# Four-bit rounding moved from GpSimd to VectorE, with more score banks and looser waits, in a transformer layer

## The chip, the cores and the metric

The program runs on all 8 cores of one Trainium2 chip. Each core computes one of the 8 sequences with all the weights, and the cores exchange nothing. The metric is the device time of one launch in microseconds, taken on the slowest core; lower is better.

## The reference

For one sequence `x` of 2048 tokens by 1024 features the layer is attention after a layer norm, then a gated feed-forward block after a second layer norm, both with a residual:

```
x = x + attn(layernorm(x))          # 16 heads of 64, rotary, causal, softmax, Wo
h = silu(q(xn) @ q(wg).T) * (q(xn) @ q(wu).T)      # xn = layernorm(x), inner width 2816
x = x + q(h) @ q(wd).T
def q(v):                           # along the last axis, blocks of 16
    scale = max(max|v| / 6, 1e-12)
    idx = searchsorted([0.25,0.75,1.25,1.75,2.5,3.5,5.0], |v/scale|)
    return [0,0.5,1,1.5,2,3,4,6][idx] * sign(v) * scale
```

So three weight matrices are rounded once, and the normed input and the inner activation are rounded for every token.

## The kernel before

The kernel is written engine by engine: a scheduler object collects steps for each engine in the order in which the Python code adds them, each with the semaphore values it waits for, and every engine runs its own list strictly in that order. Nothing is reordered later.

The work runs in stages. Stage A (to about 130 us) norms the 16 token tiles of 128 tokens and transposes them. Stage B is attention, eight passes over pairs of heads. A pass loads its slice of the projection weights (`wstg`, SyncE queue), casts it on VectorE, multiplies 16 tiles on TensorE (line 482, banks `psA` and `psB`), applies the rotary factors on VectorE, and transposes. Then for each of its two heads and each of four blocks of 512 queries (`qb`) it walks over `4*qb + 4` key chunks: a score matmul (line 588, banks `psC` and `psD` in turn), an exponential on ScalarE (lines 605 and 641) into one of four slots of `PT`, on the last four chunks a multiply by the causal mask on VectorE (lines 614 and 650), and a value matmul (lines 621 and 656). A score matmul runs one chunk ahead of the value matmul.

Between these steps `e1_pump` (after the projections, after `qb` 1, 2 and 3, and at the end of each head) puts one job of the weight rounding: 60 jobs of 128 x 1024 and 8 of 128 x 768, which are read from memory into `wfE`, rounded in `quant_chain`, and written back by a DMA on the GpSimd queue. The read of the next job is issued on the SyncE queue once the chain before has ended.

Stage C multiplies by `Wo` tile by tile (line 768), with the output in `psO` for even tiles and in `psA`/`psB` for odd ones, adds the residual on VectorE (lines 785, 787), takes the statistics of the second norm and stores the tile. Stage E loads the rounded weights and transposes them into SBUF. Stage F is the feed-forward block, 16 token tiles: load `x_t`, norm, two chains of 128 x 512, transposes and a copy `xqT_t`, then six chunks of the inner width, five of 512 and one of 256. A chunk has eight gate and eight up matmuls (1042, 1050), two ScalarE reads of them (1061, 1067), the product `hmat` on VectorE (1073), and a chain. The tail of a chunk (transposes 1001, the copy `hqT_t` 1009, eight down matmuls into `psO`, 1020) is put behind the next chunk's gate and up matmuls, and behind its chain in the lists of ScalarE. At the end of the tile `x_t + psO` is formed (1090) and stored.

`quant_chain` is the helper behind all 68 chains of stage B and all 128 of stage F. On VectorE it takes the block maxima (154) while ScalarE takes absolute values (157), forms the scales (162 to 171) and the scaled magnitude `u` (178). Its step `c3A` (187 to 194) has seven comparisons of `u` with a threshold and the sign factor. GpSimd adds the seven results in six additions (200 to 214), and VectorE multiplies by scale and sign (221 to 237) when GpSimd is done.

Of the kernel before, what the change touches and what calls it, by code (L numbers as in the profile page):

```python
# [61 lines left out]
def build_nc(debug=False):  # L62
# [31 lines left out]
    R = "right"  # L94
# [18 lines left out]
    sPOOL = Sem(root.enter_context(nc.semaphore("sPOOL")))  # L113
# [33 lines left out]
    def quant_chain(bufs, F, src, soff, dst, doff, waits1, waits3):  # L147
        (qu, qt_, qa, qb_, qc_, sg, s2, bm, sh, rb, bmc, rb2, xsq, p6, p7) = bufs
# [50 lines left out]
        def pl1(g):
            g.tensor_tensor(qa[:, 0:F], qa.ap()[:, 0:F], qb_.ap()[:, 0:F],  # L200
                            Alu.add)
            g.tensor_tensor(qc_[:, 0:F], qc_.ap()[:, 0:F], qt_.ap()[:, 0:F],  # L202
                            Alu.add)
            return g.tensor_tensor(xsq[:, 0:F], xsq.ap()[:, 0:F],  # L204
                                   p6.ap()[:, 0:F], Alu.add)
        p1v = sch.add("gpsimd", pl1, waits=[(sDVE, va)], inc=sPOOL)

        def pl2(g):
            g.tensor_tensor(qa[:, 0:F], qa.ap()[:, 0:F], qc_.ap()[:, 0:F],  # L209
                            Alu.add)  # L210
            return g.tensor_tensor(xsq[:, 0:F], xsq.ap()[:, 0:F],  # L211
                                   p7.ap()[:, 0:F], Alu.add)
        p2v = sch.add("gpsimd", pl2, waits=[(sPOOL, p1v)], inc=sPOOL)
        p3v = sch.add("gpsimd", (lambda g: g.tensor_tensor(  # L214
            qa[:, 0:F], qa.ap()[:, 0:F], xsq.ap()[:, 0:F], Alu.add)),
            waits=[(sPOOL, p2v)], inc=sPOOL)
# [14 lines left out]
        vf = sch.add("vector", c3f, waits=[(sPOOL, p3v)], inc=sDVE)  # L231
# [11 lines left out]
    with root, nc.Block() as block:  # L243
# [59 lines left out]
        for t in range(NT):  # L303
# [49 lines left out]
            if t >= 2:  # L353
# [21 lines left out]
               for i in range(2)]  # L375
# [89 lines left out]
        for pr in range(NP):  # L465
# [109 lines left out]
            for hh in range(2):  # L575
                po = 64 * hh
                for qb in range(4):
# [5 lines left out]
                    for kc in range(nkc):  # L583
                        bk = sc_ctr % 2
# [13 lines left out]
                        if len(pend) >= 2:  # L598
# [104 lines left out]
                for g in range(2):  # L703
                    def t2s(te, g=g):
# [7 lines left out]
                    wt2 = [(sDVE, vnorm), (sACT, sACT.n)]  # L712
                    t2_prev_pe = sch.add("tensor", t2s, waits=wt2, inc=sPE)
                    sch.add("scalar", (lambda c, g=g, po=po, pr=pr: c.copy(
                        attnT.ap()[po:po + 64, pr, g * 1024:(g + 1) * 1024]
                        .rearrange("p (jj f) -> p jj f", f=128),
                        psT2.ap()[0:64, :]
                        .rearrange("p (jj f) -> p jj f", f=128))),
# [19 lines left out]
        for nh in range(2):  # L738
# [15 lines left out]
        obank = [(psO.ap()[:, 0:512], psO.ap()[:, 512:1024]),  # L754
                 (psA.ap()[:], psB.ap()[:])]
        for t in range(NT):
            r = t % 2
            ob0, ob1 = obank[t % 2]
# [5 lines left out]
            def omm(te, t=t, ob0=ob0, ob1=ob1):  # L764
                ins = None
                for nh, ob in ((0, ob0), (1, ob1)):
                    for pr in range(NP):
                        te.matmul(ob,
# [3 lines left out]
                    ins = te.matmul(ob, ones1.ap(),  # L772
# [4 lines left out]
            if t >= 2:  # L777
                waits.append((sDVE, epiC[t - 2]))
# [406 lines left out]
```

How the kernel before makes its waits and increments, by code:

```python
                def f(ctx):  # L50
                    for waits, emit, inc, amt in steps:
                        for sem, val in waits:
                            ctx.wait_ge(sem.h, val)
                        ins = emit(ctx)
                        if inc is not None:
                            ins.then_inc(inc.h, amt)
# [1039 lines left out]
        def final_wait(c):  # L1096
            c.wait_ge(sFO[0].h, final_out[0])
            return c.wait_ge(sFO[1].h, final_out[1])
```

## Time and profile before

| | |
|---|---|
| median of 3 runs | 5397.76 us (5396.99 to 5398.55) |
| the profiled execution | 5398.35 us |
| span of its slowest core, from the first to the last instruction | 5396.7 us |
| spans of all cores | 5380.7 to 5396.7 us |
| busy: TensorE / VectorE / ScalarE / GpSimd | 1941.2 / 1925.0 / 1140.3 / 1875.3 us |

Busy time is that of instructions on the engine; TensorE's is modelled, as its matmuls overlap. No engine is busy for more than 36% of the span, so the shares alone don't say what sets the time: the order of the waits does. Stages by the clock of the span: A to 130 us, B to 2861, C to 2960, E to 3129, F to the end.

### The profile page before, as it was taken

Reading aid. Unit: us, or ns where it says so; the run is one execution under the profiler, and the core shown is the slowest. Engines: PE = TensorE matmul, PEld = TensorE weight load, DVE = VectorE, ACT = ScalarE, POOL = GpSimd, SP = SyncE. Lnnn points to the kernel's source line nnn. Section 1 sums busy time; section 2 is a strip of 40 time slices with the busy share of each in tenths; the row PEclk is TensorE's granted clock in tenths of the full one; section 3 lists DMA queues with packets and bytes.
Section 4 is the critical chain, followed back from the end, with each engine's and each line's share of the span. In section 5 each row is a group of like instructions: output and inputs, shape, how many; then the busy total and the mean of one; then the engine's idle time right before and its main releaser. Section 6 shows DMA issues by size and latency. Waiting matters only on the chain.

```text
span 5396.7 us, 31104 instructions; the slowest of 8 cores (5380.7 to 5396.7 us)
## 1 busy us (share of the span) xinstructions
PE 1941.2 (36%) x6864; PEld 712.1 (13%) x6864; DVE 1925.0 (36%) x4494; ACT 1140.3 (21%) x1936; POOL 1875.3 (35%) x1280
## 2 busy tenths in 40 slices
PE   1532334333323344333436333333333333333333
PEld 0101001011010011110102311111111111111111
DVE  2333332333323324243234034433334333344333
ACT  4321222212212223132222321111111111111111
POOL 0243442433434423334230034343343433443433
PEclk9656556555565565655657566666666666666666
DMA  2000000010000000000004300000000000000000
GB/s 80 22 24 30 18 24 24 24 35 18 24 29 18 23 29 22 28 22 21 23 23 161 108 24 4 8 8 8 8 8 8 8 8 8 8 8 8 8 8 4
DMA packets 49107, 131.59 MB, mean 24 GB/s; under 512 B 8610, under 2 KB 16930, under 8 KB 48803
## 3 DMA queue, kind: packets, MB, share of 16 engines
q1 hardware_dynamic: 39012, 95.51, 6.2%
q0 software_dynamic: 9920, 34.09, 1.6%
q8 instruction: 68, 1.11, 0.1%
q14 instruction: 107, 0.88, 0.1%
HBM read 95.50 MB, written 34.08 MB: 24 GB/s over the span
## 4 chain that ended last, share of the span: by engine, by line
POOL 34%; DVE 29%; PE 16%; issue 8%; ACT 7%; DMA 5%; DVEq 1%; POOLq 0%; ACTq 0%; SPq 0%
POOL qcA L214 3%; POOL qcA L209 3%; POOL qcA L200 3%; POOL qcAF L214 3%; POOL qcAF L209 3%; POOL qcAF L200 3%; POOL qxs L204 3%; POOL qxs L211 3%; POOL qcC L202 3%; POOL qxsF L204 3%; POOL qxsF L211 3%; POOL qcCF L202 3%; PE psO L621 2%; PE psA L482 2%; PE psB L482 2%
## 5 line engine op out<-in xcount | busy, mean ns | idle before, releaser
L200 POOL TENSOR_TENSOR qcA<-qcA,qcB 128x1024 f32<-128x1024 f32 (+1 forms) x68 | 154.1, 2266 | 1628.2 <-DVE qs L194 1628.2
L200 POOL TENSOR_TENSOR qcAF<-qcAF,qcBF 128x512 f32<-128x512 f32 (+1 forms) x128 | 152.7, 1193 | 1383.8 <-DVE qs2F L194 1383.8
L621 PE MATMUL psO<-PT,vaug 128*65 128x512 bf16 x576 | 360.2, 625 | 637.6 <-DVE PT L614 572.4
L221 DVE TENSOR_TENSOR qcCF<-qcAF,qshF 128x256 f32<-128x256 f32 (+1 forms) x128 | 52.3, 409 | 970.0 <-POOL qcAF L214 970.0
L221 DVE TENSOR_TENSOR qcC<-qcA,qsh 128x512 f32<-128x512 f32 (+1 forms) x68 | 46.0, 676 | 956.5 <-POOL qcA L214 956.5
L605 ACT ACTIVATE PT<-psC,nb 128x512 bf16<-128x512 f32 x320 | 219.9, 687 | 694.9 <-PE psC L588 694.6
L1001 PE MATMUL psT<-idn_b,hqb 128*128 128x128 bf16 x352 | 52.7, 299 | 804.3 <-DVE qbmF L154 720.4
L1020 PE MATMUL psO<-wdqT,hqT_t 128*128 128x512 bf16 x704 | 310.6, 618 | 77.2 <-ACT hqT_t L1009 63.2
L980 PE MATMUL psT<-idn_b,xqb 128*128 128x128 bf16 x128 | 16.2, 306 | 603.0 <-DVE xqb L237 603.0
L614 DVE TENSOR_TENSOR PT<-PT,mskb 128x512 bf16<-128x512 bf16 x192 | 77.8, 422 | 355.5 <-ACT PT L605 355.5
L482 PE MATMUL psA<-wqkvp,xlT 128*128 128x384 bf16 x512 | 108.0, 360 | 263.0 <-DVE wqkvp L471 262.9
L588 PE MATMUL psC<-QTr,KTr 64*128 64x512 bf16 x320 | 192.9, 603 | 10.7 <-ACT KTr L570 10.7
L621 PEld LDWEIGHTS psO<-PT,vaug 128*65 128x65 bf16 x576 | 75.1, 130 | 914.9 <-issue 914.9
L588 PE MATMUL psD<-QTr,KTr 64*128 64x512 bf16 x320 | 194.9, 609 | 0.0
L605 ACT ACTIVATE PT<-psD,nb 128x512 bf16<-128x512 f32 x256 | 176.0, 688 | 80.0 <-PE psD L588 79.4
L157 ACT ACTIVATE qxsF<-hmat 128x512 f32<-128x512 f32 x96 | 57.2, 596 | 625.4 <-DVE hmat L1073 625.4
L708 PE MATMUL psT<-idn_b,attokn 128*64 128x128 bf16 x256 | 33.0, 310 | 419.4 <-DVE attokn L699 399.3
L178 DVE TENSOR_TENSOR quE<-qxs,qr 128x1024 f32<-128x1024 f32 (+1 forms) x68 | 81.1, 1193 | 235.6 <-ACT qxs L157 234.0
L209 POOL TENSOR_TENSOR qcAF<-qcAF,qcCF 128x512 f32<-128x512 f32 (+1 forms) x128 | 152.7, 1193 | 18.9 <-POOL qxsF L204 0.9
L214 POOL TENSOR_TENSOR qcAF<-qcAF,qxsF 128x512 f32<-128x512 f32 (+1 forms) x128 | 152.7, 1193 | 18.3
L214 POOL TENSOR_TENSOR qcA<-qcA,qxs 128x1024 f32<-128x1024 f32 (+1 forms) x68 | 154.6, 2274 | 10.1 <-POOL qxs L211 0.5
L209 POOL TENSOR_TENSOR qcA<-qcA,qcC 128x1024 f32<-128x1024 f32 (+1 forms) x68 | 154.7, 2274 | 9.8
(184 smaller groups left out, 5034.4 us busy)
## 6 DMA issues: line engine op xcount, KB each, us to landing
wstg<-wqkv SPq DMA_DIRECT2D x8, 1536.0 KB, 8.8
wfE<-wg SPq DMA_DIRECT2D x22, 512.0 KB, 3.8
wfE<-wu SPq DMA_DIRECT2D x22, 512.0 KB, 3.9
x_a<-x SPq DMA_DIRECT2D x16, 512.0 KB, 3.5
wfE<-wd SPq DMA_DIRECT2D x16, 512.0 KB, 4.0
x_c<-x SPq DMA_DIRECT2D x16, 512.0 KB, 4.0
xscr<-x1b POOLq DMA_DIRECT2D x16, 512.0 KB, 3.6
x_t<-xscr SPq DMA_DIRECT2D x16, 512.0 KB, 3.9
```

The lines of the kernel that those rows point to most:

```text
L200: g.tensor_tensor(qa[:, 0:F], qa.ap()[:, 0:F], qb_.ap()[:, 0:F], Alu.add)
L202: g.tensor_tensor(qc_[:, 0:F], qc_.ap()[:, 0:F], qt_.ap()[:, 0:F], Alu.add)
L204: return g.tensor_tensor(xsq[:, 0:F], xsq.ap()[:, 0:F], p6.ap()[:, 0:F], Alu.add)
L209: g.tensor_tensor(qa[:, 0:F], qa.ap()[:, 0:F], qc_.ap()[:, 0:F], Alu.add)
L211: return g.tensor_tensor(xsq[:, 0:F], xsq.ap()[:, 0:F], p7.ap()[:, 0:F], Alu.add)
L214: p3v = sch.add("gpsimd", (lambda g: g.tensor_tensor(qa[:, 0:F], qa.ap()[:, 0:F], xsq.ap()[:, 0:F], Alu.add)), waits=[(sPOOL, p2v)], inc=s ...
L221: v.tensor_tensor(qc_.ap()[:, 0:F2].rearrange("p (b k) -> p b k", k=16), qa.ap()[:, 0:F2].rearrange("p (b k) -> p b k", k=16), sh.ap()[:, ...
L482: te.matmul(ps[:, 0:384], xlT.ap()[:, kc, t * 128:(t + 1) * 128], wqkvp.ap()[:, kc, :], start=(kc == 0), stop=False)
L588: return te.matmul(ps[:], KTr.ap()[po:po + 64, kc * 128:(kc + 1) * 128], QTr.ap()[po:po + 64, qb * 512:(qb + 1) * 512], start=True, stop=True)
L605: c.activation(PT[:, kcp % 4, :], ps[:], AFT.Exp, bias=nb12.ap(), scale=0.125)),
L621: return te.matmul(av_banks[abk], vaug.ap()[:, kcp, hh, :], PT[:, kcp % 4, :], start=(kcp == 0), stop=(kcp == nkc - 1), skip_group_check=True)
L1020: ins = te.matmul(psO[:, nh * 512:(nh + 1) * 512], hqT_t.ap()[:, j, :], wdqT.ap()[:, j, nh * 512:(nh + 1) * 512], start=(j == 0), stop=(j ...
```

## The change

It has five parts. (1) In `quant_chain` GpSimd's three steps are gone. `c3A` becomes `c3a` with two comparisons and the sign factor, and the other five thresholds are folded in by `scalar_tensor_tensor` instructions on VectorE, each of which compares `u` with an immediate and adds a second tensor; seven of them stand in four steps, each of which waits for the one before. The buffers `p6` and `p7` and the semaphore `sPOOL` go. (2) In attention the scores rotate over four banks (`psC`, `psD`, `psA`, `psB`), and the score matmuls run two chunks ahead. (3) The transposes in attention, and those in the feed-forward block, wait for the last ScalarE copy that read their bank, in place of the newest ScalarE step. (4) Stage C has one output bank pair, `psO`, for every tile, and one addition of 1024 columns in place of two of 512. (5) The final sum of stage F is written into new buffers `outb`, and the load of `x_t` no longer waits for the store of the tile two before.

```diff
-        def c3A(v):
+        def c3a(v):
             u = qu.ap()[:, 0:F]
             v.tensor_scalar(qa[:, 0:F], u, TH[0], None, Alu.is_gt)
-            v.tensor_scalar(qb_[:, 0:F], u, TH[1], None, Alu.is_gt)
-            v.tensor_scalar(qc_[:, 0:F], u, TH[2], None, Alu.is_gt)
-            v.tensor_scalar(qt_[:, 0:F], u, TH[3], None, Alu.is_gt)
-            v.tensor_scalar(xsq[:, 0:F], u, TH[4], 2.0, Alu.is_gt, Alu.mult)
-            v.tensor_scalar(p6[:, 0:F], u, TH[5], 2.0, Alu.is_gt, Alu.mult)
-            v.tensor_scalar(p7[:, 0:F], u, TH[6], 4.0, Alu.is_gt, Alu.mult)
+            v.tensor_scalar(qc_[:, 0:F], u, TH[4], None, Alu.is_gt)
             return v.tensor_scalar(s2[:, 0:F], sg[:, 0:F], 2.0, -1.0,
                                    Alu.mult, Alu.add)
...
-        p1v = sch.add("gpsimd", pl1, waits=[(sDVE, va)], inc=sPOOL)
...
+        def c3b(v):
+            u = qu.ap()[:, 0:F]
+            v.scalar_tensor_tensor(qb_[:, 0:F], u, TH[1], qa.ap()[:, 0:F],
+                                   Alu.is_gt, Alu.add)
+            return v.scalar_tensor_tensor(qt_[:, 0:F], u, TH[5],
+                                          qc_.ap()[:, 0:F],
+                                          Alu.is_gt, Alu.add)
+        vb = sch.add("vector", c3b, waits=[(sDVE, va)], inc=sDVE)
...
+        ve = sch.add("vector", (lambda v: v.scalar_tensor_tensor(
+            qa[:, 0:F], qt_.ap()[:, 0:F], 2.0, qb_.ap()[:, 0:F],
+            Alu.mult, Alu.add)), waits=[(sDVE, vd)], inc=sDVE)
...
-        vf = sch.add("vector", c3f, waits=[(sPOOL, p3v)], inc=sDVE)
+        vf = sch.add("vector", c3f, waits=[(sDVE, ve)], inc=sDVE)
...
-        sc_banks = [psC, psD]
+        sc_banks = [psC, psD, psA, psB]
...
+                    elif last_t2_evac[0]:
+                        waits.append((sACT, last_t2_evac[0]))
...
-                        bk = sc_ctr % 2
+                        bk = sc_ctr % 4
...
-                        if len(pend) >= 2:
+                        if len(pend) >= 3:
...
-                    wt2 = [(sDVE, vnorm), (sACT, sACT.n)]
+                    wt2 = [(sDVE, vnorm)]
+                    if last_t2_evac[0]:
+                        wt2.append((sACT, last_t2_evac[0]))
...
-        obank = [(psO.ap()[:, 0:512], psO.ap()[:, 512:1024]),
-                 (psA.ap()[:], psB.ap()[:])]
...
-            if t >= 2:
-                waits.append((sDVE, epiC[t - 2]))
+            if t >= 1:
+                waits.append((sDVE, epiC[t - 1]))
...
+            epiC[t] = sch.add("vector", (lambda v, t=t, r=r: v.tensor_tensor(
+                x1b[r][:], x_c[r][:], psO[:], Alu.add)), waits=epw, inc=sDVE)
...
-                wx.append((sFO[r], out_dma[t - 2]))
...
-            wtx = [(sDVE, q2), (sACT, sACT.n)]
+            wtx = [(sDVE, q2)]
+            if last_psT_evac[0]:
+                wtx.append((sACT, last_psT_evac[0]))
...
-                wth = [(sDVE, qh), (sACT, sACT.n)]
+                wth = [(sDVE, qh)]
+                if last_psT_evac[cset]:
+                    wth.append((sACT, last_psT_evac[cset]))
...
-                x_t[r][:], x_t[r][:], psO[:], Alu.add)), waits=epw, inc=sDVE)
-            out_dma[t] = dma("gpsimd", sFO[r], out_v[:, t, :], x_t[r][:],
+                outb[r][:], x_t[r][:], psO[:], Alu.add)), waits=epw, inc=sDVE)
+            out_dma[t] = dma("gpsimd", sFO[r], out_v[:, t, :], outb[r][:],
```

## Rows read from the trace of the kernel before

**Rows 1.** Busy time by stage, microseconds: B, then F (windows; the columns first).

```profile
core 7: us, PE busy (x) PEld busy (x) DVE busy (x) ACT busy (x) POOL busy (x), PEclk, DMA share, GB/s
130.00:2861.00 2731.00, 1035.51 (x3200) 320.44 (x3200) 943.71 (x1684) 697.94 (x1285) 956.95 (x476) 0.54 0.08 24
...
3129.00:5397.00 2268.00, 751.11 (x2720) 302.70 (x2720) 889.57 (x2544) 288.33 (x450) 909.67 (x784) 0.63 0.02 8
```

**Rows 2.** The page's chain that ended last, by engine.

```profile
POOL 34%; DVE 29%; PE 16%; issue 8%; ACT 7%; DMA 5%; DVEq 1%; POOLq 0%; ACTq 0%; SPq 0%
```

**Rows 3.** Groups on VectorE by line and shape: busy, mean ns | idle before, releaser.

```profile
L178 DVE TENSOR_TENSOR quF<-qxsF,qr2F 128x512 f32<-128x512 f32 x112 | 77.5, 692 | 20.4 <-DVE qr2F L171 19.2 <-ACT up L1067 1.0 <-ACT hqT_t L1009 0.2
L178 DVE TENSOR_TENSOR quE<-qxs,qr 128x1024 f32<-128x1024 f32 x60 | 73.5, 1225 | 229.2 <-ACT qxs L157 227.7 <-DVE qr L171 1.2 <-ACT PT L605 0.3
...
L221 DVE TENSOR_TENSOR qcCF<-qcAF,qshF 128x256 f32<-128x256 f32 x112 | 47.6, 425 | 893.9 <-POOL qcAF L214 893.9
...
L221 DVE TENSOR_TENSOR qcC<-qcA,qsh 128x512 f32<-128x512 f32 x60 | 41.5, 692 | 866.7 <-POOL qcA L214 866.7
```

**Rows 4.** One 128 x 512 chain in stage F (timeline): start, length, engine.

```profile
4021.27 0.69 DVE L178 TENSOR_TENSOR quF<-qxsF,qr2F 128x512 f32<-128x512 f32 x1 [0.17 <-ACT up L1067]
4022.14 0.43 DVE L187 TENSOR_SCALAR qcAF<-quF 128x512 f32<-128x512 f32 x1 [0.17 <-DVE quF L178]
4022.48 0.42 DVE L188 TENSOR_SCALAR qcBF<-quF 128x512 f32<-128x512 f32 x1
...
4024.92 1.26 POOL L200 TENSOR_TENSOR qcAF<-qcAF,qcBF 128x512 f32<-128x512 f32 x1 [17.91 <-DVE qs2F L194]
...
4032.74 0.43 DVE L221 TENSOR_TENSOR qcCF<-qcAF,qshF 128x256 f32<-128x256 f32 x1 [7.97 <-POOL qcAF L214]
```

**Rows 5.** VectorE in attention around one 128 x 1024 chain (timeline).

```profile
1277.91 1.21 DVE L154 TENSOR_REDUCE qbm<-wfE 128x64 f32<-128x1024 f32 x1
1279.23 0.20 DVE L162 TENSOR_SCALAR qbc<-qbm 128x64 f32<-128x64 f32 x1
...
1284.54 0.69 DVE L189 TENSOR_SCALAR qcC<-quE 128x1024 f32<-128x1024 f32 x1
...
1305.02 0.75 DVE L614 TENSOR_TENSOR PT<-PT,mskb 128x512 bf16<-128x512 bf16 x2
1307.67 0.43 DVE L614 TENSOR_TENSOR PT<-PT,mskb 128x512 bf16<-128x512 bf16 x1 [1.90 <-ACT PT L605]
1308.78 0.42 DVE L650 TENSOR_TENSOR PT<-PT,mskb 128x512 bf16<-128x512 bf16 x1 [0.68 <-ACT PT L641]
1309.23 1.22 DVE L154 TENSOR_REDUCE qbm<-wfE 128x64 f32<-128x1024 f32 x1
```

**Rows 6.** TensorE after the chain that lies behind qb 2 (timeline).

```profile
1113.93 0.61 PE L621 MATMUL psO<-PT,vaug 128*65 128x512 bf16 x1 [9.58 <-DVE PT L614]
```

**Rows 7.** One chunk of stage F, from chain end to chunk ready (timeline).

```profile
4034.29 0.68 DVE L1073 TENSOR_TENSOR hmat<-silu,up 128x512 f32<-128x512 f32 x1
4035.07 0.63 ACT L157 ACTIVATE qxsF<-hmat 128x512 f32<-128x512 f32 x1 [13.90 <-DVE hmat L1073]
...
4036.52 0.59 ACT L1009 COPY hqT_t<-psT 128x512 bf16<-128x512 bf16 x1 [0.82 <-PE psT L1001]
...
4037.36 3.57 PE L1020 MATMUL psO<-wdqT,hqT_t 128*128 128x512 bf16 x8 [0.93 <-DVE qr2F L171]
...
4045.36 0.69 ACT L1067 ACTIVATE up<-psB,rstd_all 128x512 f32<-128x512 f32 x1 [1.04 <-PE psB L1050]
```

**Rows 8.** TensorE in stage C, first matmuls of two successive tiles (timeline).

```profile
2894.66 1.90 PE L768 MATMUL psO<-wos,attnT 128*128 128x512 bf16 x8
...
2898.96 1.90 PE L768 MATMUL psA<-wos,attnT 128*128 128x512 bf16 x8
```

**Rows 9.** The 1024-column addition from psO, in stage F (timeline).

```profile
4112.40 1.22 DVE L1090 TENSOR_TENSOR x_t<-x_t,psO 128x1024 f32<-128x1024 f32 x1 [3.27 <-PE psO L1020]
```

**Rows 10.** DMA issues of the page: KB each, us to landing.

```profile
wfE<-wu SPq DMA_DIRECT2D x22, 512.0 KB, 3.9
```

More of the change, by code:

```diff
@@ L194, in c3A @@
             return v.tensor_scalar(s2[:, 0:F], sg[:, 0:F], 2.0, -1.0,
                                    Alu.mult, Alu.add)
-        va = sch.add("vector", c3A, waits=[(sDVE, v2)] + list(waits3),
+        va = sch.add("vector", c3a, waits=[(sDVE, v2)] + list(waits3),
                      inc=sDVE)
[L199 to L205, printed above, removed]
@@ L206, in quant_chain @@
-        p1v = sch.add("gpsimd", pl1, waits=[(sDVE, va)], inc=sPOOL)
[L208 to L216, printed above, removed]
+        def c3b(v):
[5 more added lines that the diff above has]
+                                          Alu.is_gt, Alu.add)
@@ new lines, in quant_chain, with c3c @@
+        vb = sch.add("vector", c3b, waits=[(sDVE, va)], inc=sDVE)
+        def c3c(v):
+            u = qu.ap()[:, 0:F]
+            v.scalar_tensor_tensor(qa[:, 0:F], u, TH[2], qb_.ap()[:, 0:F],
+                                   Alu.is_gt, Alu.add)
+            return v.scalar_tensor_tensor(qc_[:, 0:F], u, TH[6],
+                                          qt_.ap()[:, 0:F],
+                                          Alu.is_gt, Alu.add)
+        vc = sch.add("vector", c3c, waits=[(sDVE, vb)], inc=sDVE)
@@ new lines, in c3d @@
+        def c3d(v):
+            u = qu.ap()[:, 0:F]
+            v.scalar_tensor_tensor(qb_[:, 0:F], u, TH[3], qa.ap()[:, 0:F],
+                                   Alu.is_gt, Alu.add)
+            return v.scalar_tensor_tensor(qt_[:, 0:F], u, TH[6],
+                                          qc_.ap()[:, 0:F],
+                                          Alu.is_gt, Alu.add)
+        vd = sch.add("vector", c3d, waits=[(sDVE, vc)], inc=sDVE)
+        ve = sch.add("vector", (lambda v: v.scalar_tensor_tensor(
+            qa[:, 0:F], qt_.ap()[:, 0:F], 2.0, qb_.ap()[:, 0:F],
+            Alu.mult, Alu.add)), waits=[(sDVE, vd)], inc=sDVE)
@@ L711, in t2s @@
                         return ins
-                    wt2 = [(sDVE, vnorm), (sACT, sACT.n)]
+                    wt2 = [(sDVE, vnorm)]
+                    if last_t2_evac[0]:
+                        wt2.append((sACT, last_t2_evac[0]))
                     t2_prev_pe = sch.add("tensor", t2s, waits=wt2, inc=sPE)
[L714 to L718, printed above, removed]
+                    last_t2_evac[0] = sch.add("scalar", (
+                        lambda c, g=g, po=po, pr=pr: c.copy(
+                            attnT.ap()[po:po + 64, pr,
+                                       g * 1024:(g + 1) * 1024]
+                            .rearrange("p (jj f) -> p jj f", f=128),
+                            psT2.ap()[0:64, :]
+                            .rearrange("p (jj f) -> p jj f", f=128))),
                         waits=[(sPE, t2_prev_pe)], inc=sACT)
@@ L762, in build_nc, with omm @@
             wxd = dma("sync", sXC[r], x_c[r][:], x_v[:, t, :], waits=wx)
-            def omm(te, t=t, ob0=ob0, ob1=ob1):
+            def omm(te, t=t):
                 ins = None
-                for nh, ob in ((0, ob0), (1, ob1)):
+                for nh in range(2):
                     for pr in range(NP):
-                        te.matmul(ob,
+                        te.matmul(psO[:, nh * 512:(nh + 1) * 512],
                                   attnT.ap()[:, pr, t * 128:(t + 1) * 128],
@@ L771, in omm @@
                                   start=(pr == 0), stop=False)
-                    ins = te.matmul(ob, ones1.ap(),
+                    ins = te.matmul(psO[:, nh * 512:(nh + 1) * 512],
+                                    ones1.ap(),
                                     bos.ap()[:, nh * 512:(nh + 1) * 512],
@@ L922, in build_nc @@
         hqT_t = mksb(stF, "hqT_t", [128, NJ, 128], BF16, side=R)
+        outb = [mksb(stF, f"outb{i}", [128, D], F32, side=R) for i in range(2)]
         FQ2 = 512
@@ L949, in build_nc @@
         u_last = [0, 0]
+        last_psT_evac = [0, 0]
         chain_last_tr = {}
```

21 lines of the change are left out of this document (6 added, 15 removed).

## The prediction, on record before the changed kernel ran

> **What bounds the kernel now.** I read the stages first. Attention with the weight rounding (B, 2731 us) and the feed-forward block (F, 2268 us) hold 93% of the span, and in neither is any engine busy for 41% of it [rows 1]. So the bound is not an engine but a chain of handovers, and the second view to read is the chain that ended last: GpSimd 34%, VectorE 29%, TensorE 16% [rows 2]. The reader is to see that an engine which only adds seven small tensors is the largest part of it.
>
> The third view is VectorE's groups with the idle time before them. In front of line 221, the first step after GpSimd's additions, VectorE sits idle 893.9 us over 112 chains of 128 x 512 and 866.7 us over 60 chains of 128 x 1024 [rows 3], that is 7.98 and 14.44 us a chain. Both lie on a line in the width: 0.01262 us a column, so 11.2 us at 768 columns (8 chains) and 4.75 us at 256 (16 chains).
>
> The fourth view is the timeline, to see whether that idle time is on the path. In F it is plain. `u` starts at 4021.27, GpSimd starts at 4024.92, VectorE resumes at 4032.74, and the next chunk's product follows the chain directly, at 4034.29 [rows 4, 7], although that chunk's matmuls had long been read. The six chunks are a serial loop on VectorE plus GpSimd. In B a chain holds VectorE from 1277.91 to 1305.02, 27.1 us, and the causal masks of the next query block stand behind it in the same queue [rows 5]. TensorE is then idle until the mask comes. The shortest such idle time is behind `qb` 2, whose successor has 12 unmasked chunks to work on: still 9.58 us [rows 6]. In the places with nothing to overlap (end of a head, rotary step) the whole chain is on the path. I therefore take all 68 chains of B and all 128 of F to be on the path, as long as a chain isn't shortened by more than 9.58 us.
>
> **Part 1, the chain.** Removed on VectorE: five comparisons. One 128 x 512 comparison starts 0.34 us after the one before (4022.14, 4022.48) [rows 4]. At 1024 columns its length is 0.69 instead of 0.43 us [rows 4, 5], so its pitch is 0.34 + 0.26 = 0.60; at 768 and 256 columns 0.47 and 0.21. Removed with GpSimd: the idle time above. Added: seven two-input instructions. The trace of before has no `scalar_tensor_tensor`. The nearest row is VectorE's own f32 `tensor_tensor` of the same shape and operands in SBUF: 0.692 us at 512 and 1.225 us at 1024 columns [rows 3], 0.533 us for each 512 columns, so 0.96 at 768 and 0.43 at 256. I take that. Bounds: below, the one-input comparison (0.42 us at 512 columns) [rows 4], above, GpSimd's addition of the same shape (1.26 us) [rows 4]. Two instructions in one step overlap by about 0.08 us (pitch 0.34 for a length of 0.42), and a step that waits for the one before starts 0.11 us after its end (1277.91 + 1.21 to 1279.23) [rows 4, 5].
>
> New time from the end of the sign factor to line 221, at 512 columns: 0.11 + 3 pairs of (0.61 + 0.69 + 0.11) + 0.69 + 0.11 = 5.14 us, in place of 7.98. At 1024: 0.11 + 3 x (1.145 + 1.225 + 0.11) + 1.225 + 0.11 = 8.89 in place of 14.44. Saved in a chain:
> - 512: 7.98 - 5.14 + 5 x 0.34 = 4.53 us, x112 = 507
> - 256: 4.75 - 3.28 + 5 x 0.21 = 2.5 us, x16 = 40
> - 1024: 14.44 - 8.89 + 5 x 0.60 = 8.57 us, x60 = 514
> - 768: 11.2 - 7.0 + 5 x 0.47 = 6.5 us, x8 = 52
>
> Together 547 us in F and 566 us in B, 1113 us. The saving of 8.57 is under the 9.58 us of idle TensorE [rows 6], so even the best covered chain gives it in full, with 1.0 us to spare.
>
> **What TensorE must now keep up with in F.** The loop of a chunk was 16.12 us and becomes 16.12 - 4.53 = 11.6 us. In that time the tail of the chunk before and the gate and up matmuls two chunks on must be done. The chunk's product started at 4034.29, and the up values were ready at 4045.36 + 0.69 = 4046.05 [rows 7], 11.76 us later. Part 3 takes some of it back: the copy `hqT_t` started at 4036.52 because the transposes waited for the absolute values to end, at 4035.70 [rows 7]. With the looser wait the transposes are done by then, and the copy can start when ScalarE is free, 0.82 us earlier. So the values are ready after 10.94 us, and with a handover of 0.25 us (4037.11 to 4037.36) [rows 7] after 11.2, against 11.6. VectorE still sets the pace, by 0.4 us. Without part 3 TensorE would be late by about 0.4 us. Cost: nothing, covered by the chain; if the cover goes, see the second rival.
>
> **Part 2, score banks and lookahead.** After a chain two rounds of score, exponential and mask followed in series, 1305.02 to the end of the last mask at 1309.20; one round is 1308.78 - 1307.67 = 1.11 us [rows 5]. Two chunks ahead, one round is left. That is worth 1.1 us in each of 64 query blocks, 70 us at most. But behind `qb` 2 and 3 the next chain stands right behind the masks, and it needs a tile whose DMA is issued only when the chain before ends and lands 3.9 us later [rows 10]; it started 4.2 us after that end (1309.23) [rows 5]. The gain turns into a wait for that DMA. I count the other 32 blocks, and a little more for `qb` 1, which has no chain in front: 40 us (bounds 0 and 77).
>
> **Part 4, stage C.** Two tiles' matmuls start 4.30 us apart, without a gap [rows 8]. With one output pair the next tile must wait for the addition of 1.22 us [rows 9] and two handovers of 0.25: 1.7 us more, x15 = 26 us lost.
>
> **Parts 3 and 5, the rest.** The transposes in attention waited for steps that had ended, so nothing. The load of `x_t` still waits for the sum of the tile before, and that is the later of its two events; the store of two tiles before is over 100 us old. Nothing. `outb` is written in place of `x_t`, at the same length. On GpSimd's queue only the stores are left; each was issued behind the chain and is so still.
>
> **Sum.** 1113 + 40 - 26 = 1127 us. The profiled execution took 5398.35 us (span 5396.7), the median of the runs is 5397.76, 0.6 us lower. So 5397.8 - 1127 = 4270 us.
>
> A rule of the Trainium skill speaks against the price of the seven instructions. The page "Vector Engine (DVE) Microarchitecture Reference", section "Points that are easy to get wrong", says that a scalar-tensor-tensor whose two SBUF sources are not bf16 runs at half throughput. No row of before shows one, so the trace neither bears it out nor refutes it; its time is the third rival's.
>
> **The rivals.** (1) Forecast: VectorE's serial chain stays the bound, a fused instruction costs what a `tensor_tensor` costs: 4270.
>
> (2) TensorE becomes the bound in F. Its clock sits between levels there (granted 0.63 on the mean, so partly 1.2 and partly 2.4 GHz) [rows 1]. Eight matmuls of 512 columns that began after 6 us of idle took 3.57 us [rows 7]. If all three groups run so, the values are ready at 4036.54 + 3 x 3.57 + 0.8 + 0.25, 14.0 us after the product, 2.4 us late. Four chunks a tile, 16 tiles: 154 us, so 4424. For it: the margin is only 0.4 us. Against: TensorE would idle less between bursts than now, which does not speak for a lower clock.
>
> (3) The fused instruction takes twice as long per column. The seven together have 941 us of column time over all chains (7 x (60 x 1.067 + 8 x 0.80 + 112 x 0.533 + 16 x 0.267)), so 4270 + 941 = 5211. For it: GpSimd's two-input addition shows that such a price exists. Against: a compare with an immediate needs no third read, and the two tensors are read as in line 178.
>
> (4) B is covered by other work, and only F gains: 4270 + 566 = 4836. Against it stand the 9.58 us.
>
> (5) Slower than before: one mechanism, the fused instruction at more than 2.2 times the column time of line 178's (1127/941 = 1.2 on top). At three times it would be 4270 + 1882 = 6152. Nothing in the rows speaks for it but that the instruction is unseen.
>
> **How the numbers follow.** Chances: forecast 0.80, (2) 0.09, (3) 0.06, (4) 0.03, (5) 0.02. The range holds (1) with its bounds and reaches to (2): low 4190 (the whole gain of part 2, 37 us, and some 40 us if handovers or TensorE's exposed bursts come out shorter), high 4420. A difference within 0.2% (11 us) is about what a measurement of this kernel can't tell from none. Only a price near 2.2 lies there: same 0.01, slower 0.02, faster 0.97.
>
> **What would show it.** GpSimd's busy time falls from 1875 us to under 60 (its DMA issues). Each of the seven instructions: 0.69 us at 512, 1.22 at 1024 columns; at 1.2 and 2.3 the third rival holds. Successive `hmat` products in F lie 11.6 us apart; if VectorE waits there for `up`, the second. The wait of the value matmul behind `qb` 2 falls from 9.6 to about 1 us. Waits for `wfE` grow by about 1 us in two blocks of four. Tiles of stage C lie 6 us apart. What would make it wrong: a fused instruction priced otherwise, or a clock that falls when TensorE's work gets denser.

## The result, and the profile after

The changed kernel took 4244.99 us (median of 8 runs, 4241.13 to 4259.12) against 5398.10 us for the kernel before, run beside it (5396.91 to 5407.01). The ratio is 0.7864, with a 95% interval of 0.7855 to 0.7873. The forecast was 4270 us, 25 us (0.6%) too high, and the range of 4190 to 4420 held the time.

The first view is again the windows by stage, which answer to [rows 1] (B, C, E, F; the columns are those of [rows 1]):

```profile
129.00:2242.00 2113.00, 1013.40 (x3200) 319.19 (x3200) 1293.06 (x1820) 691.95 (x1286) 36.83 (x68) 0.56 0.10 31
2242.00:2364.00 122.00, 72.15 (x288) 25.95 (x288) 55.77 (x130) 22.96 (x49) 8.51 (x16) 0.89 0.49 172
2364.00:2533.00 169.00, 67.08 (x528) 50.91 (x528) 0.00 (x0) 68.43 (x69) 0.00 (x0) 0.50 0.35 103
2533.00:4244.00 1711.00, 729.47 (x2720) 294.43 (x2720) 1240.94 (x2800) 280.33 (x449) 8.50 (x16) 0.67 0.03 10
```

GpSimd's 910 us in F have become 8.5 us, its 16 stores. VectorE's busy time rose by 351 us in F, and still the stage is 556 us shorter: VectorE works more and waits less. The page says the same of the whole span in two lines, busy time and the chain that ended last (compare [rows 2], where GpSimd held 34%):

```profile
PE 1898.3 (45%) x6864; PEld 702.8 (17%) x6864; DVE 2624.6 (62%) x4870; ACT 1125.9 (27%) x1936; POOL 54.0 (1%) x104
...
DVE 54%; PE 20%; issue 9%; DMA 8%; ACT 7%; DVEq 1%; SPq 0%; ACTq 0%; POOLq 0%
```

I took the lengths of the stages from the first DMA issues on SyncE that belong to each (B from the first `wstg`, C from `wostg`, E from `ebuf`, F from the first `x_t`), in this kernel and in every run below, to compare them on one footing. They differ from [rows 1] only in rounding. Each length is that of the slowest core; within one execution the eight cores lie up to 13 us apart in B and up to 8 us in F.

| us | B | C | E | F |
|---|---|---|---|---|
| before | 2731.8 | 98.5 | 169.4 | 2267.2 |
| after | 2112.3 | 122.4 | 168.9 | 1711.2 |
| saved | 619.5 | -23.9 | 0.5 | 556.0 |
| forecast | 606 | -26 | 0 | 547 |

**The price of a fused instruction.** The groups on VectorE, by line and shape, beside the `tensor_tensor` whose price I had given them ([rows 3]):

```profile
L213 DVE SCALAR_TENSOR_TENSOR qcBF<-quF,qcAF 128x512 f32<-128x512 f32 x112 | 77.5, 692 | 12.4 <-DVE qcCF L206 0.9
L177 DVE TENSOR_TENSOR quF<-qxsF,qr2F 128x512 f32<-128x512 f32 x112 | 77.5, 692 | 20.1 <-DVE qr2F L170 20.1
L177 DVE TENSOR_TENSOR quE<-qxs,qr 128x1024 f32<-128x1024 f32 x60 | 73.5, 1225 | 219.5 <-ACT qxs L156 213.7 <-DVE qr L170 5.0 <-ACT PT L612 0.9
L220 DVE SCALAR_TENSOR_TENSOR qcA<-qtE,qcB 128x1024 f32<-128x1024 f32 x60 | 73.5, 1225 | 6.2
L227 DVE TENSOR_TENSOR qcCF<-qcAF,qshF 128x256 f32<-128x256 f32 x112 | 47.6, 425 | 11.6
```

692 ns against 692, and 1225 against 1225. The section on the change has all seven compare; in truth six do, and the seventh (L220) doubles one partial sum and adds the other. It costs the same. The step behind the additions (L227, the one that was L221) is idle for 11.6 us over 112 chains where it was idle for 893.9.

**One chain in F** (timeline of VectorE, the stretch that answers to [rows 4]):

```profile
3315.87 0.29 DVE L188 TENSOR_SCALAR qs2F<-qsgF 128x512 bf16<-128x512 bf16 x1
3316.26 0.69 DVE L195 SCALAR_TENSOR_TENSOR qcBF<-quF,qcAF 128x512 f32<-128x512 f32 x1
3316.87 0.69 DVE L197 SCALAR_TENSOR_TENSOR qtF<-quF,qcCF 128x512 f32<-128x512 f32 x1
3317.66 0.69 DVE L204 SCALAR_TENSOR_TENSOR qcAF<-quF,qcBF 128x512 f32<-128x512 f32 x1
...
3320.45 0.69 DVE L220 SCALAR_TENSOR_TENSOR qcAF<-qtF,qcBF 128x512 f32<-128x512 f32 x1
3321.25 0.42 DVE L227 TENSOR_TENSOR qcCF<-qcAF,qshF 128x256 f32<-128x256 f32 x1
```

The sign factor (L188) ends at 3316.16 and L227 starts at 3321.25: 5.09 us, forecast 5.14. Two in one step lie 0.61 us apart (3316.26, 3316.87), and the next step starts 0.10 us after the end of the second.

**One chunk in F** (timeline of three engines, as in [rows 7]):

```profile
3334.41 0.68 DVE L1082 TENSOR_TENSOR hmat<-silu,up 128x512 f32<-128x512 f32 x1
3334.74 0.38 PE L1007 MATMUL psT<-idn_b,hqb 128*128 128x128 bf16 x4 [2.15 <-DVE hqb L243]
3335.18 0.63 ACT L156 ACTIVATE qxsF<-hmat 128x512 f32<-128x512 f32 x1 [1.80 <-DVE hmat L1082]
3335.72 0.57 ACT L1017 COPY hqT_t<-psT 128x512 bf16<-128x512 bf16 x1
...
3336.43 3.56 PE L1029 MATMUL psO<-wdqT,hqT_t 128*128 128x512 bf16 x8 [1.31 <-ACT hqT_t L1017]
...
3339.80 1.92 PE L1051 MATMUL psC<-wgqT,xqT_t 128*128 128x512 bf16 x8
...
3343.55 0.69 ACT L1076 ACTIVATE up<-psD,rstd_all 128x512 f32<-128x512 f32 x1 [1.04 <-PE psD L1059]
...
3345.96 0.69 DVE L1082 TENSOR_TENSOR hmat<-silu,up 128x512 f32<-128x512 f32 x1
```

The products lie 11.6 us apart (3334.41, 3345.96), as forecast, and VectorE doesn't wait for `up`: it was ready at 3344.24, 1.7 us ahead of the product that reads it. In the next chunk it was ready 0.7 us ahead.

**Attention.** VectorE around a chain of 128 x 1024 (timeline, as [rows 5]):

```profile
1021.83 1.21 DVE L153 TENSOR_REDUCE qbm<-wfE 128x64 f32<-128x1024 f32 x1
...
1039.96 0.75 DVE L621 TENSOR_TENSOR PT<-PT,mskb 128x512 bf16<-128x512 bf16 x2
1040.63 0.42 DVE L657 TENSOR_TENSOR PT<-PT,mskb 128x512 bf16<-128x512 bf16 x1
1042.61 0.42 DVE L657 TENSOR_TENSOR PT<-PT,mskb 128x512 bf16<-128x512 bf16 x1 [1.56 <-ACT PT L648]
1044.12 1.22 DVE L153 TENSOR_REDUCE qbm<-wfE 128x64 f32<-128x1024 f32 x1 [1.09 <-DMA wfE<-wu]
```

The chain holds VectorE for 18.1 us in place of 27.1. Three masks, not two, have their chunk ready at its end. The last mask ends 3.07 us behind the chain, not 4.2, and then the chain that follows waits 1.09 us for its tile: the predicted change of one wait for another. Behind `qb` 2 TensorE's wait is now 1.76 us (1.64 to 2.00 in the twelve places with a chain of 1024 columns), where [rows 6] had 9.58 and the forecast said about 1:

```profile
1062.51 0.61 PE L628 MATMUL psO<-PT,vaug 128*65 128x512 bf16 x1 [1.76 <-DVE PT L621]
```

**Stage C.** The second half of one tile's matmuls, the addition, and the first half of the next tile's (timeline; [rows 8] shows first halves):

```profile
2291.16 1.90 PE L776 MATMUL psO<-wos,attnT 128*128 128x512 bf16 x8
...
2293.63 1.22 DVE L792 TENSOR_TENSOR x1b<-x_c,psO 128x1024 f32<-128x1024 f32 x1 [2.25 <-PE psO L780]
2294.99 1.89 PE L776 MATMUL psO<-wos,attnT 128*128 128x512 bf16 x8 [1.61 <-DVE x1b L792]
```

TensorE waits 1.61 us for the addition (of the length that [rows 9] gave it). The next tile's second half, not shown, starts at 2297.13, so the tiles lie 5.97 us apart; the forecast said 6.

The last view is VectorE's waits (engine and line, what it waited for, us in total, times, longest). It shows what is left, and so what the experiments go for:

```profile
DVE qbmF L153 <- ACT xl2c L968: 250.4, 15, 176.0
DVE PT L621 <- ACT PT L612: 233.6, 56, 15.7
DVE quE L177 <- ACT qxs L156: 218.2, 32, 30.7
DVE hmat L1082 <- ACT up L1076: 146.8, 16, 10.1
DVE PT L657 <- ACT PT L648: 95.7, 92, 2.1
DVE wqkvp L476 <- DMA wstg<-wqkv: 82.3, 8, 12.2
...
DVE qbm L153 <- DMA wfE<-wg: 24.9, 15, 3.3
DVE qbm L153 <- DMA wfE<-wu: 24.0, 15, 2.9
...
DVE qbm L153 <- DMA wfE<-wd: 19.6, 12, 3.0
```

### The profile page after: what moved, and what is told of

It is laid out like the page before. It is cut to its first block, busy times and chain, and to the rows that moved or that the text cites. A ratio compares the mean times of both kernels' runs of the same rounds, so it can differ in the third digit from the quotient of the medians.

```text
span 4244.2 us, 30489 instructions; the slowest of 8 cores (4230.1 to 4244.2 us)
## 1 busy us (share of the span) xinstructions
PE 1898.3 (45%) x6864; PEld 702.8 (17%) x6864; DVE 2624.6 (62%) x4870; ACT 1125.9 (27%) x1936; POOL 54.0 (1%) x104
## 4 chain that ended last, share of the span: by engine, by line
DVE 54%; PE 20%; issue 9%; DMA 8%; ACT 7%; DVEq 1%; SPq 0%; ACTq 0%; POOLq 0%
PE psA L487 2%; PE psB L487 2%; PE psO L628 2%; DVE qcAF L220 2%; DVE quF L177 2%; DVE qcBF L213 2%; DVE qcAF L204 2%; DVE qcBF L195 2%; DVE qbmF L153 2%; DVE qcA L220 2%; DVE quE L177 2%; DVE qcB L195 2%; DVE qcA L204 2%; DVE qcB L213 2%; DMA wstg<-wqkv 2%
## 5 line engine op out<-in xcount | busy, mean ns | idle before, releaser
L628 PE MATMUL psO<-PT,vaug 128*65 128x512 bf16 x512 | 322.6, 630 | 271.0 <-DVE PT L621 230.8
L177 DVE TENSOR_TENSOR quE<-qxs,qr 128x1024 f32<-128x1024 f32 (+1 forms) x68 | 81.2, 1194 | 224.4 <-ACT qxs L156 218.2
L153 DVE TENSOR_REDUCE qbmF<-xl2c 128x32 f32<-128x512 f32 x32 | 21.8, 681 | 250.4 <-ACT xl2c L968 250.4
L1082 DVE TENSOR_TENSOR hmat<-silu,up 128x512 f32<-128x512 f32 x96 | 61.5, 640 | 146.8 <-ACT up L1076 146.8
L1051 PE MATMUL psA<-wgqT,xqT_t 128*128 128x512 bf16 x384 | 135.4, 516 | 21.7 <-ACT xqT_t L992 21.7
L1029 PEld LDWEIGHTS psO<-wdqT,hqT_t 128*128 128x128 bf16 x704 | 86.9, 133 | 256.6 <-issue 251.6
L612 ACT ACTIVATE PT<-psC,nb 128x512 bf16<-128x512 f32 x160 | 109.9, 687 | 52.3 <-PE psC L595 52.2
L153 DVE TENSOR_REDUCE qbm<-wfE 128x64 f32<-128x1024 f32 (+1 forms) x68 | 80.6, 1185 | 68.5 <-DMA wfE<-wg 24.9
L612 ACT ACTIVATE PT<-psD,nb 128x512 bf16<-128x512 f32 x160 | 110.0, 687 | 39.2 <-PE psD L595 38.9
L879 PE MATMUL psT<-idn_b,ebuf 128*128 128x128 bf16 x528 | 67.1, 306 | 105.9 <-DMA ebuf<-wgq_raw 27.5
L724 ACT COPY attnT<-psT 64x1024 bf16<-64x1024 bf16 x32 | 32.2, 1006 | 297.5 <-PE psT L715 297.5
L648 ACT ACTIVATE PT<-psB,nb 128x512 bf16<-128x512 f32 x64 | 44.1, 689 | 249.5 <-PE psB L595 249.5
```

Of the source, the lines that this page charges most:

```text
L153: return v.tensor_reduce(bm[:, 0:nb], sv, AX.X, Alu.max, apply_absolute_value=True)
L177: return v.tensor_tensor(qu.ap()[:, 0:F].rearrange("p (b k) -> p b k", k=16), xsq.ap()[:, 0:F].rearrange("p (b k) -> p b k", k=16), rbb, A ...
L612: c.activation(PT[:, kcp % 4, :], ps[:], AFT.Exp, bias=nb12.ap(), scale=0.125)),
L628: return te.matmul(av_banks[abk], vaug.ap()[:, kcp, hh, :], PT[:, kcp % 4, :], start=(kcp == 0), stop=(kcp == nkc - 1), skip_group_check=True)
L879: ins = te.transpose(pst[:, jj * 128:(jj + 1) * 128], ebuf[r][:, (j0 + jj) * 128:(j0 + jj + 1) * 128], idn[:])
L1029: ins = te.matmul(psO[:, nh * 512:(nh + 1) * 512], hqT_t.ap()[:, j, :], wdqT.ap()[:, j, nh * 512:(nh + 1) * 512], start=(j == 0), stop=(j ...
```

## The experiments

Each is a whole kernel that computes the reference in full. Ratios are to the kernel before in the same group of runs (medians 5401.40, 5403.22 and 5403.97 us), with their 95% intervals. Lengths of stages come from one profiled execution each, cut as in the table above.

**Parts of the change alone: e1 and e2.** `e1_chain_only` is the kernel before with part 1 alone; `e2_score_only` is the kernel before with part 2 alone:

```diff
-        sc_banks = [psC, psD]
+        sc_banks = [psC, psD, psA, psB]
...
-                        bk = sc_ctr % 2
+                        bk = sc_ctr % 4
...
-                        if len(pend) >= 2:
+                        if len(pend) >= 3:
```

> The kernel before with part 1 alone (seven additions and compares as fused instructions on VectorE, GpSimd's three steps gone). Theory: the removed handover is worth 566 us in B and 547 in F; without the looser wait the copy of hqT_t comes 0.82 us later, and the up values are ready 11.76 + 0.25 us after the chunk's product, against a loop of 11.6, so TensorE's side is late by 0.4 us in 64 chunks, 26 us back: 5398 - 1113 + 26 = 4311 us, with waits of VectorE for the up values inside the tile. Rival: in the changed kernel TensorE's bursts are shorter than assumed, and VectorE still sets the pace without the looser wait: 4285 us or a little less, stage F as long as in the changed kernel.

> The kernel before with part 2 alone (four score banks, two chunks ahead), GpSimd's additions kept. Theory: 1.1 us in each of the 32 query blocks with no weight chain right behind their masks plus a little for qb 1, about 40 us: 5358 us; the waits of the weight chains for the DMA of wfE grow by about 1 us in the blocks behind qb 2 and 3. Rival one: the gain is there in all 64 blocks: 5328 us. Rival two: the lookahead was covered by the long chains and gives nothing: 5398 us.

e1: 4290.24 us, 0.7945 (0.7933 to 0.7957). B 2170.8, C 109.7, F 1718.0. The expected 4311 us did not come; the rival's 4285 is near. Part 1 takes 561 us out of B (forecast 566) and 549 out of F (forecast 547). F is only 6.8 us longer than with the whole change, where my reason for part 3 asked for 26. Its waits for `up` are

```profile
DVE hmat L1080 <- ACT up L1074: 151.6, 26, 10.2
```

26 times, against 16 in the changed kernel, and those 16 are the first chunk of each tile. So ten chunks are late on this core, by some 0.5 us each, not all 64. It is one of four cores that ran part of this stage at a lower granted clock (the last section has it); on cores 4 to 7, which did not, the waits are 19 to 22, so three to six chunks are late.

e2: 5349.56 us, 0.9906 (0.9891 to 0.9921), between the expected 5358 and the first rival's 5328. B is 50.4 us shorter, forecast 40. The gain is under 1%, but the interval is clear of 1, and it comes with GpSimd's chains still in place.

**One part undone: e3, e4, e5.** `e3_two_pairs` puts stage C's two output pairs back:

```diff
+        obank = [(psO.ap()[:, 0:512], psO.ap()[:, 512:1024]),
+                 (psA.ap()[:], psB.ap()[:])]
...
-            if t >= 1:
-                waits.append((sDVE, epiC[t - 1]))
+            if t >= 2:
+                waits.append((sDVE, epiC[t - 2]))
```

`e4_old_wait` gives only the transposes of stage F's chunks their old wait, and `e5_one_ahead` keeps the four banks but looks one chunk ahead:

```diff
-                wth = [(sDVE, qh)]
-                if last_psT_evac[cset]:
-                    wth.append((sACT, last_psT_evac[cset]))
+                wth = [(sDVE, qh), (sACT, sACT.n)]
```

```diff
-                        if len(pend) >= 3:
+                        if len(pend) >= 2:
```

> The changed kernel with part 4 undone: stage C again alternates psO with psA and psB, with two additions of 512 columns. Theory: the one bank pair costs 1.6 us a tile, so stage C goes from 122 back to about 98 us and the time to 4221. Rival: the tile's load or its statistics would set the pace once TensorE doesn't; then less than 10 us comes back.

> The changed kernel, but the transposes of the inner chunks in stage F again wait for the newest ScalarE step. Theory: the up values come 0.8 us later and VectorE waits about 0.4 us in 64 chunks: 4245 + 26 = 4271 us, seen as idle time in front of the product inside a tile. Rival: the cover is wider than I worked out (the changed kernel shows up values ready 0.7 to 1.7 us before the product), so nothing changes: 4245 us.

> The changed kernel with its four score banks, but score matmuls only one chunk ahead. Theory: the gain of part 2 is that of the depth and not of the banks; stage B goes from 2112 to about 2112 + 40 to 53 us, the time to 4285 to 4298. Rival: the banks themselves give it (a score matmul no longer waits for the exponential two back), and the time stays at 4245.

e3: 4223.80 us, 0.7821 (0.781 to 0.7833), C 98.2 us. The 24 us come back whole in the stage, and the time is 21 us shorter; part 4 is a plain loss here.

e4: 4249.78 us, 0.7866 (0.7853 to 0.7879). F is 6.8 us longer, the same as in e1. The time itself can't tell 5 us from none (within 0.2%), the stage and the count of waits can:

```profile
DVE hmat L1080 <- ACT up L1074: 150.2, 20, 10.1
```

The 26 us are refuted. Four chunks are late, and less than half of the 6.8 us is in the chunks: the stretches from the first to the last product of a tile, summed over the 16 tiles, are 930.4 to 931.6 us long on the eight cores, against 928.2 to 929.1 in the changed kernel. That is 2 to 3 us. Most of the rest lies ahead of the first product of a tile, a stretch in which the cores of one execution of the changed kernel already differ by 5 us (535.2 to 540.0).

e5: 4315.52 us, 0.7993 (0.7977 to 0.8009), above the expected 4285 to 4298. B is 58.8 us longer, C and F as in the changed kernel within about 2 us. The time is 70.5 us longer, and B on the median of the eight cores 64.0: so part 2's gain is 59 to 71 us, depending on how it is taken, and more than expected each time. B is as long as in e1 (2171.1 against 2170.8), which has two banks, so all of the gain is the depth, and four banks without it give nothing. Its waits of VectorE, for the masks and for the tile, are

```profile
DVE PT L621 <- ACT PT L612: 361.4, 130, 16.9
...
DVE PT L657 <- ACT PT L648: 43.7, 64, 1.0
...
DVE qbm L153 <- DMA wfE<-wg: 14.9, 9, 3.1
DVE qbm L153 <- DMA wfE<-wu: 14.6, 9, 2.9
DVE qbm L153 <- DMA wfE<-wd: 13.2, 8, 3.0
```

The waits for the tile are 42.7 us in 26, where the changed kernel has 68.5 in 42; those of the two mask lines are 405.1 us, where it has 329.3. Part 2 turns 25.8 us of its gain into this wait, as the prediction said of the blocks behind `qb` 2 and 3, but less than the 35 us (32 x 1.1) that it took off.

**The waits that are left: e6 to e8.** `e6_early_wfe` lets the read of the next weight tile wait for the chain two back, which is the last that used this buffer, not for the newest one. `e7_early_xt` lets the load of `x_t` wait for the sum two tiles back. `e8_all` is both with e3.

```diff
-            ws = ([(sDVE, e1["prev_chain"])] if ji >= 1
+            ws = ([(sDVE, e1["prev2"])] if ji >= 2
...
+            e1["prev2"] = e1["prev_chain"]
             e1["prev_chain"] = qv
```

```diff
             if t >= 2:
-                wx.append((sDVE, prev_epi))
+                wx.append((sDVE, epi_of[t - 2]))
```

> The changed kernel, but the read of the next weight tile waits for the chain two back (the last reader of its buffer) in place of the newest chain. Theory: the waits of the weight chains for wfE (68.5 us) go, and as the SyncE queue is no longer held by that wait, the read of the next projection weights, which stands behind it, starts during the last chain of a pass instead of after it; of the 82 us of idle time in front of the cast some 66 go too: 4245 - 134 = 4111 us. Rival one: the cast's wait has another cause than the queue (its own load of 1.5 MB), and only the 68 us go: 4177. Rival two: the gain turns into longer transfers or a wait of TensorE elsewhere, and less than 30 us is left.

> The changed kernel, but the load of x_t waits for the final sum of two tiles before in place of the one before, which the new output buffers allow. Theory: part 5 as it stands gives nothing, because the load waits for the sum of the tile before; with that wait moved, the load and the norm lie under the chain, and the 5.3 us of idle time before the first chain of a tile go in 14 tiles: 4245 - 75 = 4170 us. Rival: the norm is queued on ScalarE behind the last copy, and the last down matmuls and the sum hide nothing, so under 20 us is gained.

> The changed kernel with two bank pairs in stage C, the early read of weight tiles and the early load of x_t together. Theory: they lie in three stages and add up: 4245 - 24 - 134 - 75 = 4012 us. Rival: with the waits for transfers gone in stage B, TensorE and ScalarE become the bound behind qb 2, where 1 us of idle time was left, and the sum falls short by 20 us or more.

e6: 4169.10 us, 0.7716 (0.7703 to 0.773). A gain of 76 us, where I had expected 134. The number is near that of the first rival (4177), but not for its reason, for the waits of the cast did go. The waits show where it went:

```profile
DVE quE L177 <- ACT qxs L156: 279.5, 68, 33.7
...
DVE wqkvp L477 <- DMA wstg<-wqkv: 13.6, 1, 13.6
```

The waits for `wfE` are gone (68.5 us), and with them seven of the eight waits for `wstg` (82.3 to 13.6 us). The `wstg` loads stand behind the tile's read in SyncE's queue, and that read no longer holds them. But now the chain waits for the absolute values in all 68 jobs, 61 us more than before. The timeline of VectorE shows one such wait (on ScalarE, not shown, two copies into `attnT` start at 1146.78 and 1149.06, and the absolute values behind them at 1150.08, although the tile was there at 1145.32):

```profile
1145.32 1.21 DVE L153 TENSOR_REDUCE qbm<-wfE 128x64 f32<-128x1024 f32 x1
...
1151.24 1.23 DVE L177 TENSOR_TENSOR quE<-qxs,qr 128x1024 f32<-128x1024 f32 x1 [2.74 <-ACT qxs L156]
```

B fell by 85.4 us all the same; 14 of them were lost again in stage C, of which the last section tells. My theory had priced the wait that went and not the one that stood next.

e7: 4180.20 us, 0.774 (0.7726 to 0.7754), 65 us less than the changed kernel; F is 71.2 us shorter (expected 75). The norm's wait at the start of a tile goes from 250.4 us in 15 waits to one, which is stage E's:

```profile
DVE qbmF L153 <- ACT xl2c L969: 177.5, 1, 177.5
```

e8: 4063.55 us, 0.7519 (0.7506 to 0.7531). Expected was 4012. Against the changed kernel B is 91 us shorter, C 10 and F 74. So most of the miss is e6's shortfall in B (134 expected), and 14 us are stage C's, which took 112.7 us on this core and 97.0 to 98.9 on six of the others (the last section shows its clock).

**Following the moved wait: e9 and e10.** If the wait in e6 is for a place in ScalarE's line, then forming the absolute values one job ahead, in a buffer of their own, must remove it. `e9_early_abs` is e6 with this; `e10_all_abs` is e8 with it.

```diff
+            aqw = [(sWE[r], wdma)]
+            if ji >= 2:
+                aqw.append((sDVE, e1["prev2"]))
+            e1["aq_prev"][ji] = sch.add("scalar", (
+                lambda c, r=r, F=F: c.activation(
+                    xsE[r][:, 0:F], wfE[r].ap()[:, 0:F], AFT.Abs)),
+                waits=aqw, inc=sACT)
```

> The changed kernel with the early read of weight tiles, and in addition the absolute values of the next weight job are put into ScalarE's list at the pump before, into one of two buffers, so that they no longer stand behind the copies of the query block or of the projections. Theory: the early read alone took 137 us of transfer waits off VectorE but gained 80, because its waits for the absolute values rose from 218 to 280 us; with them computed a job ahead, some 50 us of that comes back, and the chain behind the projections (about 16 us of it lies behind them today, in 7 passes) runs under them, 112 us: 4167 - 162 = 4005 us, and VectorE's wait for the absolute values falls under 20 us. Rival: the missing 55 us was lost to something else, to TensorE's slower clock in stage C (14 us longer there) and to transfers, and in the query blocks nothing comes back; then only the 112 us go: 4055.

> All of the follow-ups together: two bank pairs in stage C, early read of weight tiles, early load of x_t, absolute values a job ahead. Theory: 4061 - 162 = 3899 us. Rival as for the kernel without the stage C and stage F edits: 3949 us; or TensorE's and ScalarE's own work in the query blocks becomes the bound, and more than 3950 us is left.

e9: 3997.47 us, 0.7395 (0.7383 to 0.7407), B 1858.2 us: 172 us below e6 and 8 below the expected 4005, so the rival (4055) falls. The waits:

```profile
DVE tR L534 <- ACT vaug L517: 126.0, 8, 29.9
...
DVE quE L178 <- DVE qr L171: 10.9, 63, 0.2
```

The step that makes `u` now waits for VectorE's own `qr`, and for ScalarE only 0.9 us in five waits (not shown). What comes next is the copy of the values (`vaug`) at the head of each pass, which had been 30.3 us in one wait and is 126.0 in eight.

e10: 3906.36 us, 0.723 (0.7215 to 0.7245), expected 3899. It is the fastest of all: 8.0% below the changed kernel (3906.36/4244.99), and 27.7% below the one before.

## Why the prediction was right, and where it was off

**The bound.** A chain of handovers between GpSimd and VectorE, serial in both stages: right. Part 1 alone gives 0.7945. Rival 4, that B is covered, asked for 4836; B alone gave 561 us in e1. The argument was the idle time of TensorE behind `qb` 2 [rows 6], longer than the saving. In e1, where nothing but the chain differs, 0.63 to 1.09 us of it are left in the twelve places with a chain of 1024 columns (forecast 1.0). But 9.58 us was not the shortest such time, as I had it: those twelve began at 9.22, and behind three chains of 768 columns TensorE's wait was only 4.5 us (at 2044.57, 2386.54 and 2728.02), less than the 6.5 us that such a chain was to give. There 2.35 us are left in e1. That may be why B gave 5 us less than forecast; no run tests it.

**The price of the fused instruction.** Right to the nanosecond for the first of a step (the second ones took about 684 and 1217 ns), and it was the term on which most hung. Seven of them took 5.09 us with their handovers (5.14 forecast) at 512 columns and 8.83 (8.89 forecast) at 1024, from the sign factor's end at 1028.52 to line 227 at 1037.35. With that rival 3 (5211 us) and rival 5 fall. The rule of the Trainium skill beside rival 3 ("Vector Engine (DVE) Microarchitecture Reference", section "Points that are easy to get wrong"), half throughput for a scalar-tensor-tensor with SBUF sources that aren't bf16, is not what the trace shows, if it is read against `tensor_tensor`: both took 692 ns on f32. The page doesn't say against what the half is meant. Against a one-input comparison the trace agrees with it: from 512 to 1024 columns that one grew from 426 to 694 ns and the fused one from 692 to 1225, twice as much. The measurement decides, and for this forecast the first comparison was the one that counted.

**What TensorE must keep up with.** The pace of 11.6 us was right, and rival 2 (4424) did not come. But the margin was mis-sized: I gave VectorE 0.4 us. Over the third to fifth product of each tile, 48 in all, the up values of the changed kernel were ready 0.43 to 3.7 us ahead of it, with medians of 1.2, 1.8 and 1.2 us. Most of that comes of the one chunk that I had read. In [rows 7] the values came 11.76 us after the product; the mean of the 48 in the kernel before is 11.2. That chunk's eight gate matmuls took 2.81 us (a row at 4040.72 that isn't shown there), where their mean is 2.35. In the changed kernel the values come after 10.2 us on the mean (forecast 10.94), and the copy `hqT_t` starts 1.31 us after the product where it was 2.23 (0.92 earlier, forecast 0.82). VectorE then starts 0.10 us behind the values and not 0.25. The two chunks shown, with margins of 1.7 and 0.7 us, are within the scatter, and so is the gate group of 1.92 us there: the mean is 2.42, so these matmuls got no faster.

The clock that I had named as a danger did not fall. The mean granted clock in F rose from 0.63 to 0.67. But that is mostly the shorter stage: by the clock records of the two traces TensorE stood at the full 2.4 GHz for 570 us of F before and for 591 us after, and at 1.2 GHz for the rest. Rival 2 had also misread its row: the 6 us of idle time that it names isn't there, TensorE had been idle for 15.46 us ahead of the four transposes.

**Part 3.** Right that it helps, wrong in size. "Without part 3 TensorE would be late by about 0.4 us" held for ten chunks in e1 and four in e4, and not for all 64: F is 7 us longer in both, where 26 would have followed, and in e4 only 2 to 3 us of that are in the chunks. The margin above explains it: the old wait lets the copy start 0.7 to 0.9 us later, and only those chunks are late whose margin is thinner than that.

**Part 2.** The step is right, the term too small: 40 us forecast, 50.4 in e2 and 58.8 between the changed kernel and e5. I took the gain behind `qb` 2 and 3 to vanish in the wait for the tile. VectorE's waits show what came instead: those for the masks are 75.8 us shorter than in e5 (I had counted 70 at most), those for the tile 25.8 us longer (and not 35), and those for the absolute values 7.7 us shorter (218.2 against 225.9, which isn't shown). Together that is 57.7 of the 58.8 us. It is a sum of waits in two traces, not a test of each.

**Part 4.** Right: 23.9 us lost, 26 forecast, and e3 gets them back.

**Part 5.** Right at nothing. The load of `x_t` has two waits, and the change removed the earlier one. No run undoes part 5 alone, but VectorE's wait at the start of a tile is as long in e1, which lacks it (252.4 us in 15 waits), as in the changed kernel (250.4 in 15). e7 loosened the later one and gained 71 us in F.

**The sum.** 561 + 549 for part 1, 59 for part 2 with the rest in place, 7 for part 3 and -24 for part 4 give 1152, and the stages give 1152 (619.5 + 556.0 + 0.5 - 23.9). For F that is so by construction, as the 7 are what e1 leaves; for B it is a test, as 561 and 59 come from two runs. The forecast's 1127 was 25 us short: part 2 gave 19 more, part 3, counted only as a cover, 7, part 4 cost 2 less, and part 1 gave 3 less.

## What to carry to other kernels

If an engine holds a large share of the chain that ended last but isn't busy, price the whole handover (its work, the wait there and back) against the same work in line on the engine that waits; here 7.98 us became 5.09 although VectorE got more to do. Before you price a wait that is to go, list what stands next in every queue that fed it: e6 was to gain 134 us and gained 85 in B, because VectorE's wait for a ScalarE step that had been waiting for the same DMA grew by 61, and e9 got it back, and more, by moving that step. And when a change removes a wait, check that it is the later of the two: part 5 took the earlier and gained nothing, e7 took the later and gained 71 us.

## What the runs showed of the hardware that I had not expected

In stage C, where TensorE is busiest, the granted clock is not the same in all executions and not on all cores. In the changed kernel every core stood at the full clock for 95.6 us of its stage C (0.89 on the mean). In e6, whose stage C has the same instructions, cores 4 to 7 did the same and took 122.1 to 125.5 us, but cores 0 to 3 spent 39 to 92 us of it at 0.81, between the two levels, and took 129.6 to 136.3. The window of stage C on e6's slowest core, core 2, to be set against the second row of the windows above, and 80 us out of it:

```profile
2156.00:2292.00 136.00, 86.10 (x288) 28.24 (x288) 55.81 (x130) 23.01 (x50) 8.54 (x16) 0.75 0.43 155
2210.00:2290.00 80.00, 59.72 (x207) 19.77 (x206) 37.42 (x90) 15.87 (x35) 6.40 (x12) 0.81 0.40 144
```

The same 288 matmuls took 86.10 us where they took 72.15, and that is the 14 us. The level of 0.81 is also in stage C of e1 (cores 0 and 1: 109.7 and 108.3 us, the others 97.1 to 101.1), of e8 (cores 2 and 3: 107.5 and 112.7 us, the others 97.0 to 98.9) and of e10 (cores 4 to 7: 107.7 to 110.7 us), and it stands for up to 160 us in F of these runs and of e7 and e9. In each run only cores of one die (0 to 3 or 4 to 7) have it, and the kernel before, the changed one, e2, e3, e4 and e5 have it nowhere. What sets it is open: no run here varies it. It is worth knowing that a stage that is bound by TensorE can move by 11 to 14 us, 0.3% of this kernel, with nothing changed in it.
